# Local attention layers: scores and values on 64 rows of the TensorE array each, with whole-tile evacuations in place of zero-padded ones

## The reference

```python
def local_attention(q, k, v):
    w = WINDOW                                   # 32
    ...
    bk2, bv2 = (look(bk), look(bv))              # the window before, and the window itself: 64 keys
    ...
    sim = jnp.einsum('bhwie,bhwje->bhwij', bq, bk2) * QK_SCALE
    sim = jnp.where(mask, -jnp.finfo(sim.dtype).max, sim)
    attn = jax.nn.softmax(sim, -1)
    out = jnp.einsum('bhwij,bhwje->bhwie', attn, bv2)
    return out.reshape(b, h, n, d)

for i in range(DEPTH):                           # 6
    x = attn_layer(shift_tokens(x), Wqkv[i], q_scale[i], k_scale[i], Wo[i]) + x
    x = ffn_layer(shift_tokens(x), ln_g[i], ln_b[i], W1[i], b1[i], W2[i], b2[i]) + x
```

## Time and profile before

| what | value |
|---|---|
| time, median of 3 runs | 4100.39 us (4099.25 to 4101.06) |
| the profiled execution's own time | 4098.77 us |
| its span, first to last instruction | 4096.9 us |
| mean granted TensorE clock | 0.977 |
| busy: PE, ACT, DVE, POOL | 3940.0, 3771.9, 3450.4, 2329.4 us |
| the layers run from about | 1000 to 4050 us |

### The profile page before, as it was taken

How to read it: one execution, slowest core, us unless ns; L and a number is a source line. 1 busy time by engine, 2 the same in 40 slices (tenths; PEclk the granted TensorE clock), 3 DMA queues, 4 the chain that set the end, 5 groups by cost and what they waited for, 6 DMA issues and landing times. The chain is left out here.

```text
span 4096.9 us, 125398 instructions
## 1 busy us (share of the span) xinstructions
PE 3940.0 (96%) x43636; PEld 2914.0 (71%) x43636; DVE 3450.4 (84%) x8234; ACT 3771.9 (92%) x7378; POOL 2329.4 (57%) x2684
## 2 busy tenths in 40 slices
PE   4999999997999999999999999999999999999995
PEld 2566666663777777777777777777777777777774
DVE  4788888875988888888888888888888888888884
ACT  4899999985999999999999999999999999999995
POOL 4000000006777777777777777777777777777773
PEclk7899999997999999999999999999999999999997
DMA  6777777752111111111111111111111111111111
GB/s 180 223 232 231 228 228 230 234 176 75 49 44 47 46 40 44 44 49 46 39 44 49 44 49 35 49 44 49 44 38 46 49 44 44 49 36 48 44 49 54
DMA packets 249745, 347.67 MB, mean 85 GB/s; under 512 B 45104, under 2 KB 206364, under 8 KB 249116
## 3 DMA queue, kind: packets, MB, share of 16 engines
q1 hardware_dynamic: 249244, 340.94, 27.9%
HBM read 151.06 MB, written 82.85 MB: 57 GB/s over the span
## 5 line engine op out<-in xcount | busy, mean ns | idle before, releaser
L1468 PE MATMUL la_ps<-la_Wqkv,la_xsT 128*128 128x512 f32 x2304 | 1172.8, 602 | 6.8 <-DVE X L1164 6.8
L1164 DVE TENSOR_TENSOR X<-la_ps,la_tab 128x1024 f32<-128x1024 f32 x768 | 938.2, 1222 | 102.0 <-ACT la_sq L1312 95.6
L1094 POOL TENSOR_TENSOR la_rt<-X 128x512 f32<-128x512 f32 x384 | 495.9, 1291 | 589.9 <-PE la_ps L1483 436.6
L1111 POOL TENSOR_TENSOR la_rt<-la_rt,la_rn 128x1024 f32<-128x1024 f32 x384 | 722.4, 1902 | 27.5
L1173 DVE TENSOR_REDUCE la_ssum<-la_sq 128x8 f32<-128x512 f32 x768 | 511.1, 666 | 0.0
L1312 ACT ACTIVATE la_sq<-la_ps 128x512 f32<-128x512 f32 x768 | 464.9, 605 | 34.8 <-PE la_ps L1468 30.1
L1095 POOL TENSOR_TENSOR la_rt<-X 128x512 f32<-128x512 f32 x384 | 495.6, 1291 | 0.0
L527 POOL COPY at_vh<-V 128x64 f32 (+1 forms) x64 | 15.1, 236 | 783.9 <-PE at_ps L726 782.7
L1499 PEld LDWEIGHTS la_ps<-la_kT,la_qB 128*64 128x64 f32 x12288 | 390.4, 138 | 85.1 <-issue 73.7
L1468 PEld LDWEIGHTS la_ps<-la_Wqkv,la_xsT 128*128 128x128 f32 x2304 | 362.3, 190 | 120.3 <-issue 75.3
L1499 PE MATMUL la_ps<-la_kT,la_qB 128*64 128x64 f32 x12288 | 432.9, 224 | 0.0
(11 more groups left out here) (204 smaller groups left out, 9046.2 us busy)
## 6 DMA issues: line engine op xcount, KB each, us to landing
at_band<-skew_scratch SPq DMA_DIRECT2D x64, 1536.0 KB, 7.3
la_vs<-la_v SPq DMA_DIRECT2D x192, 384.0 KB, 3.5
skew_scratch<-at_R SPq DMA_DIRECT2D x64, 1024.0 KB, 6.7
la_vs<-la_v SPq DMA_DIRECT2D x192, 128.0 KB, 3.4
la_Wqkv<-in_wqkv SPq DMA_DIRECT2D x28, 384.0 KB, 5.4
at_qh<-qt_scratch SPq DMA_DIRECT2D x64, 144.0 KB
at_kh<-kt_scratch SPq DMA_DIRECT2D x64, 144.0 KB
la_W<-in_L_ffn_W SPq DMA_DIRECT2D x24, 341.0 KB, 5.2
```

What stands on the lines that cost most here:

```text
L1094: e.tensor_tensor(dst[:, :, 0, :], c[:, :, 0, :], s[:, :, 1, :], ALU.add)
L1111: e.tensor_tensor(heads(rt, w), heads(rt, w), wide(rn[:, w * H:(w + 1) * H], D), ALU.mult)\
L1164: e.tensor_tensor(dst.rearrange("p f (h d) -> p f h d", d=D), ps[:, c % 2, :].rearrange("p (h d) -> p h d", d=D).unsqueeze(1).to_broadcast ...
L1468: e.matmul(ps[:, c % 2, :], xsT[:, m * P:(m + 1) * P], Wqkv[:, ds(layer(n) % 2, 1), c * 512:(c + 1) * 512], start=True, stop=True)\
```

## The change

- `qT` and `pT` take the place of `qB` and `pB` and hold no zeros. `q_turned` and `p_turned` are one ACT instruction of 128 partitions per bank. Two memsets on POOL go.
- A score matmul is now one head and one window: stationary 64 rows x 32 columns, moving 64 columns. The parity `par` of the head picks the row half of the array (partitions 0 to 63 or 64 to 127) and the output bank; the window and the pair pick one of four groups of 32 output partitions. 64 matmuls per tile.
- A value matmul is one head, one window and one of two groups of keys: stationary 64 rows x 64 columns (v), moving 32 columns. The row half is `wl` and picks the output bank. 64 matmuls per tile.
- Both halves of heads now share each bank. So `scores(n, m)` is one block that waits for both halves of q, k and the mask, `values(n, m)` is one block that follows it and waits for both halves of the probabilities, and each raises its semaphore once, by 2, at its end. Both `o_out` of a tile wait for the whole of `values`.
- The order within the `body` of ACT, DVE, POOL and SP is not changed.

```diff
             def q_turned(n, m, u):
-
-                src = ps[:, TURNED_Q[u], :].rearrange("p (j w q) -> p j w q", j=4, w=WPT)
                 e.wait_ge(Tq_mm.sem, Tq_mm.v(n, u + 1))
-                e.wait_ge(S_mm.sem, S_mm.v(n - 1, u + 1))
-                e.activation(qB[0:D, 4 * u:4 * u + 4, :, 0, :], src[0:D], ACT.Copy)
-                e.activation(qB[D:P, 4 * u:4 * u + 4, :, 1, :], src[D:P], ACT.Copy).then_inc(Tq_ev.sem, 1)
+                e.wait_ge(S_mm.sem, S_mm.v(n - 1))
+                e.activation(qT[:, 4 * u:4 * u + 4, :], ps[:, TURNED_Q[u], :].rearrange("p (j t) -> p j t", j=4),
+                             ACT.Copy).then_inc(Tq_ev.sem, 1)
...
-            def o_out(n, m, h):
-                e.wait_ge(pv_mm.sem, pv_mm.v(n, h + 1))
+            def o_out(n, m, l):
+                e.wait_ge(pv_mm.sem, pv_mm.v(n))
                 e.wait_ge(wo_mm.sem, wo_mm.v(n - 1))
-                e.activation(oT[:, 4 * h:4 * h + 4, :], ps[:, OUT[h], :].rearrange("p (j t) -> p j t", j=4),
+                e.activation(oT[:, :, l * D:(l + 1) * D], ps[:, OUT[l], :].rearrange("p (j t) -> p j t", j=8),
                              ACT.Copy).then_inc(o_ev.sem, 1)
...
-            def scores(n, m, h):
+            def scores(n, m):
...
-                for j in range(4):
+                for c in range(4):
                     for wl in range(2):
-                        for g in range(2):
-                            w, col = g + 2 * wl, j * P + wl * D
-                            at = m % RING_V * P + w * WIN
-                            mm = e.matmul(bank[g * D:(g + 1) * D, col:col + D], qB[:, 4 * h + j, w, :, :],
-                                          kT[:, 4 * h + j, at:at + 2 * WIN], start=False, stop=True,
-                                          skip_group_check=True)
-                mm.then_inc(S_mm.sem, 1)
+                        for jj in range(2):
+                            for g in range(2):
+                                w, at = g + 2 * wl, m % RING_V * P + (g + 2 * wl) * WIN
+                                to = slice((2 * g + jj) * WIN, (2 * g + jj + 1) * WIN)
+                                col = c * P + wl * D
+                                for par in range(2):
+                                    of = slice(par * D, (par + 1) * D)
+                                    mm = e.matmul(ps[to, BANK_S + par, col:col + D], qT[of, 2 * c + jj, w * WIN:(w + 1) * WIN],
+                                                  kT[of, 2 * c + jj, at:at + 2 * WIN], start=False, stop=True,
+                                                  skip_group_check=True)
+                mm.then_inc(S_mm.sem, 2)
...
-                            mm = e.matmul(to[:, :, g, :], keys[:, head:head + D], pB[:, pair, 2 * g + par, :, :],
-                                          start=True, stop=True, skip_group_check=True)
-                mm.then_inc(pv_mm.sem, 1)
+                            for wl in range(2):
+                                of = slice(wl * D, (wl + 1) * D)
+                                mm = e.matmul(ps[rows, OUT[wl], to:to + WIN], keys[of, head:head + D],
+                                              pT[of, 4 * par + c, at:at + WIN], start=True, stop=True, skip_group_check=True)
+                mm.then_inc(pv_mm.sem, 2)
```

More of the change, by code:

```diff
@@ L968, in layers @@
         TURNED_Q, TURNED_K, TURNED_P, OUT = (4, 5), (5, 4), (5, 4), (5, 4)
-        N_IN, SET = 7, 7
+        N_IN, SET = 7, 6
         def layer(n):
@@ L1020, in zeros @@
                 e.memset(kT[:, half, :].rearrange("p a b -> p (a b)"), 0.0).then_inc(s_set, 1)
[L1021 to L1024, removed]
         def casts(e):
@@ L1357, in p_turned @@
             def p_turned(n, m, h):
[L1358 removed]
                 e.wait_ge(pt_mm.sem, pt_mm.v(n, h + 1))
[L1360 to L1365 removed]
+                e.wait_ge(pv_mm.sem, pv_mm.v(n - 1))
+                e.activation(pT[:, 4 * h:4 * h + 4, :], ps[:, TURNED_P[h], :].rearrange("p (j c) -> p j c", j=4),
+                             ACT.Copy).then_inc(pt_ev.sem, 1)
+            def o_out(n, m, l):
+                e.wait_ge(pv_mm.sem, pv_mm.v(n))
                 e.wait_ge(wo_mm.sem, wo_mm.v(n - 1))
[L1367 removed]
+                e.activation(oT[:, :, l * D:(l + 1) * D], ps[:, OUT[l], :].rearrange("p (j t) -> p j t", j=8),
                              ACT.Copy).then_inc(o_ev.sem, 1)
@@ L1508, in turn_p, with values @@
                 mm.then_inc(pt_mm.sem, 1)
-            def values(n, m, h):
-                e.wait_ge(pt_ev.sem, pt_ev.v(n, h + 1))
+            def values(n, m):
+                e.wait_ge(pt_ev.sem, pt_ev.v(n))
                 e.wait_ge(v_ev.sem, v_ev.v(n))
                 e.wait_ge(vs_in[m % 2].sem, vs_in[m % 2].v(n // 2))
-                for j in range(4):
-                    pair = 4 * h + j
+                for pair in range(H // 2):
+                    c, jj = pair // 2, pair % 2
                     for g in range(2):
+                        keys = (vs[:, m % 2, :], v[:, m % RING_V, :])[g]
+                        at, to = (2 * g + jj) * WIN, pair * D + g * WIN
                         for par in range(2):
-                            keys = (vs[:, m % 2, :], v[:, m % RING_V, :])[g]
                             head, rows = (2 * pair + par) * D, slice(par * D, (par + 1) * D)
-                            to = ps[rows, OUT[h], j * P:(j + 1) * P].rearrange("p (l g q) -> p l g q", l=2, g=2)
-                            mm = e.matmul(to[:, :, g, :], keys[:, head:head + D], pB[:, pair, 2 * g + par, :, :],
-                                          start=True, stop=True, skip_group_check=True)
-                mm.then_inc(pv_mm.sem, 1)
+                            for wl in range(2):
[3 more added lines that the diff above has]
+                mm.then_inc(pv_mm.sem, 2)
             def out_proj(n, m):
@@ L1589, in body @@
                 for n, m in t.back(4):
-                    scores(n, m, 0)
+                    scores(n, m)
                 for n, m in t.back(5):
-                    e.wait_ge(pt_ev.sem, pt_ev.v(n, 1))
-                    e.wait_ge(Tk_ev.sem, Tk_ev.v(upto(n + 1), 1))
-                    e.wait_ge(Tq_ev.sem, Tq_ev.v(upto(n + 1), 2))
-                    e.wait_ge(o_ev.sem, o_ev.v(n - 1, 1))
-                    values(n, m, 0)
-                for n, m in t.back(4):
-                    scores(n, m, 1)
-                for n, m in t.back(5):
-                    e.wait_ge(pt_ev.sem, pt_ev.v(n, 2))
-                    e.wait_ge(Tk_ev.sem, Tk_ev.v(upto(n + 1), 2))
-                    e.wait_ge(Tq_ev.sem, Tq_ev.v(upto(n + 1), 1))
-                    e.wait_ge(o_ev.sem, o_ev.v(n - 1, 2))
-                    values(n, m, 1)
+                    e.wait_ge(Tk_ev.sem, Tk_ev.v(upto(n + 1)))
+                    e.wait_ge(Tq_ev.sem, Tq_ev.v(upto(n + 1)))
+                    e.wait_ge(o_ev.sem, o_ev.v(n - 1))
+                    values(n, m)
                 for n, m in t.back(2):
```

11 lines of the change are left out of this document (5 added, 6 removed).

## The result

| | before | after |
|---|---|---|
| time, median | 4100.7 us | 4810.0 us (4794.5 to 4812.1) |
| span of the profiled execution | 4096.9 us | 4810.3 us |
| PE busy | 500.00 of 500 us | 433 to 437 of 500 us |

The changed kernel takes **1.172 times** as long (95% interval 1.170 to 1.175). The direction was forecast, the size was not: 4810 us lies 574 us above the forecast and 390 us above the top of its range.

What follows compares the result with a forecast made beforehand. PE was taken as the bound; +0.50 us before the scores and +0.22 us from scores to `turn_q` made +0.72 us a step, x 190 = 137 us on 4098.8: 4236 us (52%), range 4110 to 4420.

Steps and rivals of the forecast that it cites:

- PE's instructions: PE issuing the score and value matmuls: can start them as fast as weight loads 7 ns apart; no term for supply.
- The values: PE's block of 64 value matmuls per tile: four tiles side by side, weight load setting the pace, 1.86 us as before.
- the 3.71 of the bound: Rival in the values: weight loads of the two row halves follow one another, 3.71 us, 4590 us in all; 12%.
- The scores: PE's block of 64 score matmuls per tile: eight tiles side by side, 0.93 us against 1.9 before.
- The rival at 1.86: Row halves or issue give the scores nothing, so they stay at 1.86 us, 4384 us in all; 13%.
- The issue rule: Skill's rule for PE: starts never closer than about 25 ns, so scores 1.6 us; the prediction held 7 ns against it.
- The gap: On PE between scores and values: change of array shape and six waits take 0.22 us, bounds 0.05 and 0.35.
- Wait one: Before the scores: all 64 need ACT's second mask, so they start 0.50 us late per step, bounds 0.43 and 0.60.
- Wait two: Both `o_out` on ACT need all values, so the distance from scores to `turn_q` grows by 0.22 us a step.
- The clock "still 1.00": PE's granted clock, expected to stay at 1.00 as in the kernel before.
- The whole: The step: first score to `turn_q` 6.03 us against 5.81 before, and 0.50 us more between `turn_k` and scores.
- 10, 5 and 12% of its own chances: Cases outside the range: both waits hidden (3972 us, 10%), wait one alone (4067 us, 5%), serial weight loads (4590 us, 12%).

Runs made afterwards that it cites:

- e2: Kernel before with each score and value matmul cut in two of 32 stationary columns, all 128 rows, order and waits untouched: 4397 us, ratio 1.073.
- e4: e3 with the scores also moved ahead of `qkv` 2 and `back_out` on PE, so these lie between scores and values: 4436 us, ratio 1.083.
- e6: e5 with the scores of the kernel before (zeros, 128 rows, 32 matmuls) and the new values: 4192 us, ratio 1.023.
- e11: e5 with the loop over the row half outermost in scores and values, so all of one row half runs first: 4843 us, ratio 1.183.
- e3: Changed kernel with only ACT's second mask moved to right behind its first: 4616 us, ratio 1.127.
- e5: e4 with the first `o_out` moved behind `exp` 0 on ACT, so both `o_out` stand together: 4284 us, ratio 1.045.
- e1: Kernel before with its own matmuls and zeros, but in the change's order and with its waits: 4575 us, ratio 1.116.
- e9: e5 with `qkv` 3 moved between the two halves of the values on PE: 4288 us, ratio 1.047.
- e10: e9 with the scores also cut in halves and `qkv` 2 between them: 4298 us, ratio 1.049.
- e12: Kernel before, halves and waits untouched, with scores on 64 rows, both row halves into one bank and different column groups: 4201 us, ratio 1.025.

## Why the prediction was wrong

- **PE's instructions: the step that failed.** "Column groups therefore run side by side and PE can issue that fast" rested on eight weight loads 7 ns apart. For eight it is true. For 256 records in 3.1 us it isn't: the packets of instructions don't follow, and PE stood 1.77 us a step, 336 us of the 709. The prediction has no term for the supply of instructions, which puts it at nothing without a reason, though the page of before shows the queue: 321 packets for 43,636 records in 4097 us. e2 shows that more records alone make the stalls, e4 that slow matmuls between the blocks shrink them, e6 that the new values alone don't have them.
- **The values**, 1.86 us: 1.85 outside the stalls. Right in size; with one row half after the other they take 3.5 us (e11), near the 3.71 of the bound. That the weight load sets this pace, the prediction's reason, was not tested.
- **The scores**, 0.93 us: 1.25. The row halves save time, but not by half. The sum carries them at 0.98, 0.05 more than their own paragraph, without a reason; against that the term is 0.28 us a step too small. The rival at 1.86 was twice as far off.
- **The issue rule.** The score records start 9.9 ns apart on average over 128, a matmul of two records every 20 ns. The Trainium skill (TensorE: Matmul & The Clock Gate, Back-to-back issue gap) has about 25 ns as the least distance; the measurement decides, and here it is lower.
- **The gap** before the values, 0.22 us: the last score starts at 2520.16 + 1.25 = 2521.41, the first value at 2521.71, 0.30; the median over all steps is 0.23. Right.
- **Wait one**, PE idle some 0.5 us, ended by ACT L1344: 0.49. Right in place and size. e3 gave back twice that, and the clock rose with it (0.94 to 0.97).
- **Wait two**, `turn_q` later though PE had less to do: PE idle 0.33 us a step ahead of L1534, and 0.59 us a step for the weight load of `turn_q`, L1469, by the view of its waits (0.36 a step before). The forecast has 6.03 - 3.00 = 3.03 us from the start of the last value to `turn_q`, where the kernel before takes 2.08; measured it is 3.13 in the median, 3.34 on average. Right in place and nearly in size: the stall delays the last value, and the chain behind it is as long as forecast. e5 gave back 152 us.
- **The clock "still 1.00"**: 0.94. Wrong. The two falls shown above come behind a stall inside the scores (after) and in slow values without a stall (e11); e1, with 1.83 us a step of idle time ahead of the scores and `turn_y`, kept 1.00. What it makes of the 709 us no run separates, but the distances between starts allow an estimate. `qkv` and `turn_q`, whose own work is unchanged, take 0.51 us a step more than before, and the values' gaps under 0.3 us some 0.3 more than at full clock (27 ns a record at 0.50, 15 at 1.00): 0.8 us a step, some 155 us.
- **The whole.** From the first score to `turn_q` it is 8.81 us, forecast 6.03; the rest of the step grew by 0.69 us, forecast 0.50. The forecast's 0.72 us a step, 1.77 of stalls, 0.28 of scores, 0.08 of the gap and 0.8 of clock add up to 3.65 of the 3.69.
- **Slips in its working.** A copy 0.61 us shorter puts wait one's upper bound at 0.56 us and not 0.60. The range leaves out 10, 5 and 12% of its own chances, so it holds 73 in 100, not 8 in 10. Neither moves the forecast.

The sum had the two waits right and was off by what PE does between them. Of the rivals, none named instructions as something to be waited for.

## What to carry to other kernels

Count instructions as a resource with a rate: where a change makes matmuls cheaper by making them more, compare the records in the longest row of cheap ones with the packets of the instruction queue, and put long matmuls between such rows. Watch too who waits for the end of a block that replaces two halves: in e9 and e10 the stalls shrank, but the last value and both `o_out` came later, and nothing was won. And test a change's order and its work apart, since three moves of order were worth 526 of 709 us.

## What the runs showed of the hardware

- **PE can run out of instructions.** One packet of 16 KB per some 130 matmul records with their loads, used 2.4 us after its start, packets at least 3.2 us apart; 256 cheap records a step with nothing slow between them stall 1.1 to 1.6 us a step; 192 hardly do (0.02 in e6, with `qkv` and `back_out` between, 0.10 in e12, in a row). The trace calls it "issue", inside a block of equal matmuls.
- **Matmuls that alternate between the two row halves of the array, each with its own bank, are faster** than the same ones with first all of one half and then all of the other: 9.9 ns a record for 13.1 in the scores, 14.6 for 27.6 in the values. In one bank, and different column groups, it was 14.0, no gain.
- **A new shape of the stationary operand costs time**: from the last value to the first score it is 0.15 us where 64 x 32 follows 128 x 64 (e12), with the same waits 0.05 where the shape stays (before) and 0.01 in e2.
- **The granted clock falls to 0.50 without PE being idle.** In e11 PE was busy for 3.90 of 4.00 us with narrow 64-row values ahead of the fall.
